# Post-norm linear attention with a butterfly FFN: x first in the load queue, contraction weights transposed in slot 13, epsilon on VectorE, one norm applied by ScalarE

## What is computed

```python
q, k, v = split(x @ W_qkv)                    # 16 heads of 64
q, k = relu(q @ W_f + b_f), relu(k @ W_f + b_f)
kv = einsum('bhnd,bhne->bhde', k, v)
o = einsum('bhnd,bhde->bhne', q, kv) / (einsum('bhnd,bhd->bhn', q, k.sum(axis=2)) + 1e-6)
x = layernorm(x + merge(o) @ W_out + b_out)   # eps 1e-5
h = butterfly(x @ W_exp + b_exp, up_weights)  # 512 wide, 9 stages of 2x2 blocks
h = butterfly(gelu(h + up_bias), down_weights)
x = layernorm(x + h @ W_con + b_con + down_bias)
```

## Time and profile before

| | us |
|---|---|
| median of 3 runs | 331.06 (330.26 to 331.89) |
| the profiled execution | 331.18 |
| its span | 329.4 |
| TensorE busy in it | 309.8 |
| VectorE busy | 244.9 |
| ScalarE busy | 153.3 |
| GpSimd busy | 105.8 |

### The profile page before, as it was taken

One profiled execution on the slowest core, in us unless ns is written; L12 is line 12 of the kernel. 1 busy time (PEld: TensorE's weight loads), 2 busy tenths in 40 slices (PEclk: granted clock), 3 DMA queues, 4 the chain that ended last, 5 costly groups with the idle time before them and its releaser, 6 DMA issues.

```text
span 329.4 us, 5508 instructions
## 1 busy us (share of the span) xinstructions
PE 309.8 (94%) x2009; PEld 233.5 (71%) x2009; DVE 244.9 (74%) x479; ACT 153.3 (47%) x273; POOL 105.8 (32%) x111
## 2 busy tenths in 40 slices
PE   5899799999989999999999999999999898999992
PEld 4666476776757777677678777777797686769892
DVE  2568999869599899788892896669747843757845
ACT  2633235444643453555362456336647846330440
POOL 4058999990000002300210033004402602423523
PEclk9999999999999999999999999999999999999999
DMA  6993335376900840460047011900191182372012
GB/s 180 245 335 98 112 127 190 119 214 155 224 0 6 196 85 1 111 150 0 3 113 148 0 35 45 215 1 0 38 225 33 37 206 52 95 169 61 1 34 64
DMA packets 25762, 33.95 MB, mean 103 GB/s; under 512 B 3944, under 2 KB 14600, under 8 KB 25736
## 3 DMA queue, kind: packets, MB, share of 16 engines
q1 hardware_dynamic: 25576, 33.57, 40.0%
q10 hardware_dynamic: 160, 0.03, 0.0%
HBM read 31.24 MB, written 2.36 MB: 102 GB/s over the span
## 4 chain that ended last, share of the span: by engine, by line
PE 71%; DVE 11%; DMA 5%; issue 4%; SPq 3%; ACT 3%; POOL 2%; POOLq 0%; DVEq 0%; ACTq 0%
PE ring L642 26%; PE kx_ps L729 13%; PE attn_ps L642 8%; PE spare_ps L832 7%; PE ring L749 4%; DMA x<-_L_ffn_down_weights_dram 3%; PE desk L651 2%; PE desk L763 2%; DMA bf_col<-in_L_attn_b_f_dram 2%; PE desk L738 2%; PE ring L709 2%; SPq L489 1%; DVE late L1195 1%; POOL rstd L587 1%; DVE qn L1309 1%
## 5 line engine op out<-in xcount | busy, mean ns | idle before, releaser
L1011 ACT ACTIVATE q<-ring,bf_col 128x512 f32<-128x512 f32 x64 | 43.8, 684 | 42.4 <-PE ring L642 41.8
L581 POOL TENSOR_TENSOR var_eps<-mean_var,ln_eps 128x4 f32<-128x4 f32 x14 | 7.1, 504 | 169.9 <-DVE mean_var L1322 169.9
L729 PE MATMUL kx_ps<-k,xs 128*128 128x512 f32 x128 | 60.1, 592 | 0.0
L1309 DVE TENSOR_TENSOR qn<-q,recips 128x512 f32<-128x512 f32 x64 | 42.4, 701 | 2.1 <-DMA recips<-recip_rows 2.1
L997 ACT ACTIVATE qn_h<-qn 128x512 fp32r<-128x512 f32 x48 | 29.5, 625 | 30.1 <-DVE qn L1309 30.1
L564 POOL TENSOR_TENSOR y<-hid,y_up 128x512 f32<-128x512 f32 x18 | 33.6, 1889 | 17.1 <-DMA hid<-in_L_ffn_up_weights_dram 16.1
L729 PEld LDWEIGHTS kx_ps<-k,xs 128*128 128x128 f32 x128 | 23.9, 189 | 17.9 <-issue 15.4
L642 PE MATMUL ring<-xT_h,wq_h 128*128 128x512 f32 x64 | 35.6, 556 | 0.2 <-ACT hid L1074 0.2
L1177 DVE TENSOR_TENSOR qn_l<-qn,qn_h 128x512 fp32r<-128x512 f32 x48 | 32.2, 679 | 4.3 <-ACT qn_h L997 4.1
L1275 DVE TENSOR_TENSOR k_total<-k_total,k 128x1024 f32<-128x1024 f32 x24 | 35.1, 1461 | 0.3
L1249 DVE TENSOR_TENSOR k<-ring,bf_minus 128x512 f32<-128x512 f32 x32 | 21.9, 684 | 14.2 <-PE ring L642 14.1
(11 more groups left out here) (174 smaller groups left out, 595.8 us busy)
## 6 DMA issues: line engine op xcount, KB each, us to landing
recips<-recip_rows SPq DMA_DIRECT2D x64, 256.0 KB, 5.5
hid<-in_L_ffn_up_weights_dram SPq DMA_DIRECT2D x9, 512.0 KB, 3.9
x<-_L_ffn_down_weights_dram SPq DMA_DIRECT2D x9, 512.0 KB, 6.6
xs<-in_L_attn_x_dram SPq DMA_DIRECT2D x4, 512.0 KB, 6.4
out_dram<-y SPq DMA_DIRECT2D x7, 256.0 KB, 2.3
q<-in_L_attn_W_qkv_dram SPq DMA_DIRECT2D x2, 512.0 KB, 8.1
q<-in_L_attn_W_qkv_dram SPq DMA_DIRECT2D x2, 256.0 KB, 3.3
q<-in_L_attn_W_out_dram SPq DMA_DIRECT2D x2, 256.0 KB, 8.9
```

What stands on the lines that cost most here:

```text
L729: t_.matmul(kx_ps[half], xs[b % XBUF][:, t, :], k[kt % KRING][:, half * CH:(half + 1) * CH], start=t == 0, stop=t == TILES - 1).then_inc(s ...
L1011: a_.activation(q[:, i % QRING, :], bank(("q", i))[:, :], ACT.Relu, bias=bf_col[:, :])\
L1309: v.tensor_tensor(qn[:, a % NRING, :], q[:, a % QRING, :], recips[:, a % PAIRS // RC, a % RC, :], ALU.mult).then_inc(s_qn, 1)
```

## The change

1. Loads: the first chunk of x is loaded ahead of the k weights, the second after SyncE has waited for the second half of the k weights. A partition takes four tokens that lie side by side (2 KB in one piece, in place of four pieces of 512 bytes); the output is stored in the same order (2 KB pieces, 1 KB for the halves of the last chunk). All x loads have the new order. `bf_row` is loaded through ScalarE's queue, and the two loads of `bf_col` stand behind the load of x for sequence 1, with a semaphore of their own that the first q relu waits for.
2. TensorE's first work: see the rows below. ScalarE's and VectorE's first work follows that order.
3. ScalarE, not VectorE, copies the transposed v weights in slots 1 and 2.
4. `down_step` 8 stands in slot 12 (was 10); its result is transposed on the desk and copied to `wdn` in slot 13 (was 16).
5. Epsilon, and the negated mean where it is needed, are made by VectorE right behind `bn_aggr`.
6. In the slot of the last norm product (277 us) the first attention step stands ahead of it.
7. The second LayerNorm of chunk 6 is applied by ScalarE after its last gelu (VectorE before, ahead of its work on the last chunk). Chunk 7 has statistics tiles of its own.

```diff
-    DOWN_STEP_SLOT = {1: 0, 2: 1, 3: 2, 5: 3, 6: 4, 7: 5, 8: 6, 9: 7, 10: 8}
+    WDN_SLOT = 13
+    DOWN_STEP_SLOT = {1: 0, 2: 1, 3: 2, 5: 3, 6: 4, 7: 5, 8: 6, 9: 7, 12: 8}
+    BY_ACT = [[n for s, n in ATT_T_SLOT.items() if s < APPLY_END],
+              [n for s, n in Y_SLOT.items() if s < APPLY_END] + [LAST - 1]]
-    xs_view = x.rearrange("b (t p) c -> b p t c", p=128)
-    out_view = out.rearrange("b (h t p) c -> (b h) p t c", p=128, h=CHUNKS)
+    xs_view = x.rearrange("b (h p t) c -> b p h t c", p=128, h=CHUNKS)
+    out_view = out.rearrange("b (h p t) c -> (b h) p t c", p=128, h=CHUNKS)
...
+            load_x(0, slice(0, 1), s_xs0)
             for half in range(2):
                 cols = slice(HD + half * CH, HD + (half + 1) * CH)
                 sp.dma_start(wqkv_raw[:, cols], W_qkv[:, cols]).then_inc(s_wk[half], 16)
-            sp.dma_start(xs[0][:, :, :], xs_view[0, :, :, :]).then_inc(s_xs[0], 16)
-            sp.dma_start(bf_row[:, :], b_f.rearrange("(o n) -> o n", o=1).to_broadcast([128, D])).then_inc(s_bf, 16)
+            sp.wait_ge(s_wk[1], 16)
+            load_x(0, slice(1, 2), s_xs[0])
             weights(0, s_wq)
-            for h in range(2):
-                sp.dma_start(bf_col[h * D:(h + 1) * D, :], b_f.rearrange("(p o) -> p o", o=1)).then_inc(s_bf, 16)
...
-                pool.wait_ge(s_mv[i], QUADS * (n + 1))
-                g.tensor_tensor(var_eps[i][:, :], mean_var[i][:, :, 1], ln_eps[:, :].to_broadcast([128, QUADS]),
-                                ALU.add).then_inc(s_ve[i], 1)
...
+                for a in adds(s)[:1]:
+                    add_attn(a)
                 if s in LATE_NORM_SLOT:
                     norm(LATE_NORM_SLOT[s])
-                for a in adds(s)[:1]:
-                    add_attn(a)
...
+                if s in V_SLOT:
+                    act.wait_ge(s_dmade, desk_of["v", V_SLOT[s]] + 1)
+                    a_.activation(wT[:, (4 + V_SLOT[s]) * CH:(5 + V_SLOT[s]) * CH], desk[:, :],
+                                  ACT.Copy).then_inc(s_dtaken, 1)
...
+            layer_norm_apply(1, LAST - 1, y[:, (LAST - 1) % 2, :, :], s_yo)
...
+                dve.wait_ge(s_mv[i], QUADS * (n + 1))
+                v.tensor_scalar(var_eps[i][:, :], mean_var[i][:, :, 1], LN_EPS, 1.0, ALU.add,
+                                ALU.mult).then_inc(s_ve[i], 1)
+                if n in BY_ACT[i]:
+                    v.tensor_scalar(mean_minus[i][:, :], mean_var[i][:, :, 0], -1.0, 0.0, ALU.mult,
+                                    ALU.add).then_inc(s_mm[i], 1)
...
-            layer_norm_end(1, LAST - 1, y[:, (LAST - 1) % 2, :, :], s_yo)
```

More of the change, by code:

```diff
@@ L274, in postln_linear_attention_butterfly_ffn_kernel @@
         x1T_l = sb("x1T_l", [128, CH], fp32r)
[L275 to L278, removed]
+        stats = [sb(f"stats{i}", [128, QUADS, 6]) for i in range(3)]
+        mean_var = [sb(f"mean_var{i}", [128, QUADS, 2]) for i in range(3)]
+        var_eps = [sb(f"var_eps{i}", [128, QUADS]) for i in range(3)]
+        rstd = [sb(f"rstd{i}", [128, QUADS]) for i in range(3)]
         mean_minus = [sb(f"mean_minus{i}", [128, QUADS]) for i in range(2)]
@@ L380, in postln_linear_attention_butterfly_ffn_kernel @@
         s_atc = sem("attn_copied")
[L381 to L384, removed]
+        s_st = [sem(f"stats_{i}_done") for i in range(3)]
+        s_mv = [sem(f"mean_var_{i}_done") for i in range(3)]
+        s_ve = [sem(f"var_eps_{i}_done") for i in range(3)]
+        s_rs = [sem(f"rstd_{i}_done") for i in range(3)]
+        s_mm = [sem(f"mean_minus_{i}_done") for i in range(2)]
         s_of = [sem(f"offset_{i}_done") for i in range(2)]
@@ L465, in _ @@
             load_down(0)
-            sp.dma_start(xs[1][:, :, :], xs_view[1, :, :, :]).then_inc(s_xs[1], 16)
+            load_x(1, slice(0, CHUNKS), s_xs[1])
+            for h in range(2):
+                sp.dma_start(bf_col[h * D:(h + 1) * D, :], b_f.rearrange("(p o) -> p o", o=1)).then_inc(s_bfc, 16)
             load_down(1)
@@ L864, in _ @@
             fold_wf(3, spare_ps)
[L865 to L871, removed]
+            pe.wait_ge(s_wh, 1)
+            pe.wait_ge(s_wl, 1)
             for s in range(SLOTS):
@@ L1075, in gelu @@
                     .then_inc(s_taken, 1)
+            act.wait_ge(s_xp, 1)
+            hi(xT_h[:, 0, 0:CH], kx_ps[0], s_xTh)
             act.wait_ge(s_wT, 1)
             a_.activation(wT[:, 2 * CH:3 * CH], ring[0][:, :], ACT.Copy).then_inc(s_wTa, 1)
-            for half, fold in enumerate([attn_ps, spare_ps]):
-                act.wait_ge(s_fold, half + 1)
-                hi(wk_h[:, half * CH:(half + 1) * CH], fold[:, :], s_wh)
-            act.wait_ge(s_xp, 1)
-            hi(xT_h[:, 0, 0:CH], kx_ps[0], s_xTh)
-            act.wait_ge(s_bf, 48)
+            act.wait_ge(s_fold, 1)
+            hi(wk_h[:, 0:CH], attn_ps[:, :], s_wh)
+            act.wait_ge(s_bf, 16)
             act.wait_ge(s_bfz, 1)
@@ L1121, in _ @@
                 if s == 0:
-                    for half, fold in enumerate([attn_ps, spare_ps]):
+                    act.wait_ge(s_wT, 3)
+                    a_.activation(wT[:, CH:2 * CH], attn_ps[:, :], ACT.Copy).then_inc(s_wTa, 1)
+                    k_relu(1, 0)
+                    for half, fold in enumerate([spare_ps, attn_ps]):
                         act.wait_ge(s_fold, half + 3)
@@ L1432, in _ @@
                     layer_norm_end(1, Y_SLOT[s], y[:, Y_SLOT[s] % 2, :, :], s_yo)
-                if s in V_SLOT:
-                    dve.wait_ge(s_dmade, desk_of["v", V_SLOT[s]] + 1)
-                    v.tensor_copy(wT[:, (4 + V_SLOT[s]) * CH:(5 + V_SLOT[s]) * CH], desk[:, :]).then_inc(s_dtaken, 1)
                 if s == WCON_SLOT:
@@ L1448, in _ @@
                     bias_row_step(st)
+                if s == WDN_SLOT:
+                    dve.wait_ge(s_dmade, desk_of["wdn",] + 1)
+                    v.tensor_copy(wdn[:, :, :].rearrange("p a c -> p (a c)"), desk[:, :]).then_inc(s_dtaken, 1)
                 if s == BIAS_T_SLOT:
```

102 lines of the change are left out of this document (58 added, 44 removed).

## The result

The changed kernel took 329.16 us (median of 11 runs, 327.75 to 331.22); the kernel before, run on the same chips, 331.89 (11 runs, 329.72 to 335.33). The ratio is 0.992, with a 95% interval from 0.990 to 0.995: faster, by 2.7 us. The forecast was 326.5 with a range from 324.0 to 328.9, so the time lies outside it and the gain is little more than half of the 4.65 forecast. (The forecast was laid on an execution of 331.18; laid on the 331.89 of the kernel before here, the same gain would have given 327.2, still 1.9 too low.) The profiled execution took 328.99, its span is 327.2 (329.4 before): 2.2 us less.

What follows compares the result with a forecast made beforehand. The prediction took TensorE, busy 309.8 of 329.4 us, to bound the kernel. Its terms, 2.5 + 1.4 + 0.45 - 0.4 + 0.7 = 4.65 us off an execution of 331.18, gave 326.5 us, range 324.0 to 328.9.

Steps and rivals of the forecast that it cites:

- TensorE ready for `ksum`: Slot 14: TensorE would reach ksum at 109.0 us, against 112.77 in the kernel before.
- the new wait there: At ksum of slot 14, TensorE would wait about 1.2 us for VectorE, which copies wdn until 110.2.
- early at `ksum`: Slot 14: counted through VectorE alone, TensorE would be early by 112.77 - 110.2 = 2.5 us.
- slot 16: The transposition of wdn at 135.06 and the wait behind it, to 136.44, both go: 1.4 us gained.
- epsilon in the middle: Epsilon on VectorE, 0.23 to 0.4 us per norm, lies in time TensorE doesn't wait for: taken as nothing.
- late norm order: Attention step ahead of the last norm product fills TensorE's 0.87 us wait at 277.44; 0.45 us gained, bounds 0 and 0.9.
- epsilon ahead of the first half norm: Three epsilon additions on VectorE before chunk 7's first half norm (311.49), which TensorE waits for: 0.4 us lost.
- the end: VectorE takes chunk 7 without first applying chunk 6's norm, and a GpSimd wait shrinks by 0.3: 0.7 us gained.
- TensorE stays at half speed: Rival on the start: doubled product spacing lasts on, to 26 us for a measurable loss, 332.8 us; chance 0.05.
- the 1.0 of the start: Start: 1.4 us of waits removed, less a load-queue gap, taken as 1.0; said not to enter the time at ksum.
- Step 5: VectorE's down-butterfly step, waiting for its load, would start 0.8 us earlier than 70.48, at about 69.7.
- rival C: Slower case: doubled spacing of TensorE's products in the start lasts until 26 us, giving 332.8 us; chance 0.05.

Runs made afterwards that it cites:

- e1: Changed kernel with the transposition and copy of wdn in slot 15 in place of 13; 326.88 us (4 runs), ratio to the kernel before 0.986.
- e3: Changed kernel with both the desk wait and the thin products of slot 14's ksum moved behind the second k product; 326.16 us (4 runs).
- e2: Changed kernel with the desk wait left in place, but the 16 thin products of slot 14's ksum behind the second k product; 328.13 us (4 runs).
- e4: Changed kernel with epsilon and the negated mean made by GpSimd, as in the kernel before; 327.49 us (10 runs).
- e8: Changed kernel without SyncE's wait for the k weights ahead of the second chunk of x; 332.88 us (one run).
- e10: Changed kernel with the v weights copied off the desk by VectorE again, in place of ScalarE; 335.62 us (one run).
- e7: Changed kernel with x and the output in the old token order, pieces of 512 bytes in every load and store; 330.18 us (one run).
- e11: Kernel before with only step 8 moved to slot 12 and wdn to slot 13; 336.26 us (one run).
- e6: Changed kernel with VectorE's copy of wdn ahead of the bias step in slot 13, to shorten the wait at ksum; 328.50 us (one run).
- e5: Changed kernel with wdn in slot 15 and epsilon on GpSimd; 325.15 us (4 runs), ratio to the kernel before 0.978.
- e9: Changed kernel with slot 14's desk wait and thin ksum products behind the second k product, and epsilon on GpSimd; 324.69 us (5 runs), ratio 0.977.

## Why the prediction was wrong, step by step

| step | forecast | measured |
|---|---|---|
| TensorE ready for `ksum` (a time) | 109.0 | 108.56 |
| the new wait there (in the next row) | 1.2 | 1.51 |
| early at `ksum` | 2.5 | 2.70 |
| fall of the clock behind it | 0 | -1.70 |
| slot 16 | +1.4 | +1.48 |
| epsilon in the middle | 0 | -0.93 |
| late norm order | +0.45 | +0.39 |
| epsilon ahead of the first half norm | -0.4 | -0.46 |
| the end | +0.7 | +0.72 |
| sum | 4.65 | 2.2 |

From the third row on, each measured value is the difference of one instruction's start in the two traces, less the difference at the instruction of the row above.

**The step that failed** is the one with the new wait: "TensorE is early by 112.77 - 110.2 = 2.5". The time of `ksum` was right (110.07 for 110.2 and 0.1 of semaphore); what it is worth was not: of the 2.70 us 1.0 was left at the transposition of the bias. I charged the wait only for its length, as if TensorE went on behind it as fast as before. It went on at half clock for 3.4 us from 113.2 on. A row to suspect it was there: in the start the second fold takes 1.22 us where the first takes 1.92, and the rival "TensorE stays at half speed" used just that. I did not ask whether the speed can drop again at the wait that I was adding. e1 and e3 took the wait away and the fall went with it, and e2 shows that what stands next to the wait counts. With this term the sum is 2.95. The Trainium skill (TensorE: Matmul & The Clock Gate, HAM oscillation) tells of a kernel in which TensorE waits for loads between bursts of products, is throttled by it, and starts the next burst cold. The traces here agree that the clock can fall after a wait; but these waits were of 0.6 to 1.5 us and for a copy, and the clock fell 0.6 to 3.1 us behind them, not at the first product. Why thin products next to the wait matter, and why some executions of e4 escape, stays open.

**The second step** is "I take nothing" for epsilon in the middle. I argued from "TensorE stands nowhere in 160 to 250 us", but the cover of a VectorE operation is VectorE's own slack, and VectorE's rows show no wait from 214.8 to 231.4 and from 248.4 to 262 us. TensorE then waits for it, 0.20 at 227.18 and 0.29 at 252.03: the prediction had named such waits (between 140 and 250 us) as a sign that it is wrong. The price of a norm was in my numbers (0.23 to 0.4; it is 0.27 here); the collision with GpSimd wasn't. e4 gives back 0.4 by 227 us and 1.0 by 261; the 0.93 of the table is what the two traces lose against each other between 143 and 262 us.

**Right for a wrong reason.** The wait at `ksum` came out at nearly the forecast length, and I wrote "this value comes from VectorE alone: the 1.0 of the start doesn't enter it". It does. VectorE in the changed kernel (lines far apart, between 68 and 110 us):

```profile
68.20 1.16 DVE L1221 TENSOR_TENSOR late<-x,spare_ps 128x512 f32<-128x512 f32 x1 [2.07 <-DMA x<-_L_ffn_down_weights_dram]
...
80.19 1.29 DVE L1335 TENSOR_TENSOR qn<-q,recips 128x512 f32<-128x512 f32 x2 [1.03 <-DMA recips<-recip_rows]
...
94.28 0.69 DVE L1275 TENSOR_TENSOR k<-ring,bf_minus 128x512 f32<-128x512 f32 x1 [1.04 <-PE ring L651]
...
96.50 0.95 DVE L1319 RECIPROCAL recip<-recip 128x128 f32<-128x128 f32 x1 [0.33 <-ACT recip L1066]
...
109.35 0.67 DVE L1480 COPY wdn<-desk 128x512 f32<-128x512 f32 x1
```

Step 5 stood at 68.20, 1.5 earlier than I had it, and the reciprocals' step 1.7 earlier; then, without step 8 in slot 10, VectorE caught up and waited 1.04 for TensorE at 94.28. From the reciprocal of slot 12 it has 12.8 us of work to the copy of `wdn` in every trace that has the copy at that place (96.50 to 109.35; 98.77 to 111.61 in e8; 101.51 to 114.34 in e10), and TensorE has 1.5 less to `ksum`. So the wait is 1.5 whenever TensorE comes: with the start 2.3 later (e8) it is 1.52, with slot 2 slower (e10) 1.50. Nor does the load of step 5 set it: step 5 stood at 68.20 in the changed kernel, at 69.68 in e4 and at 71.10 in e7, and the wait was 1.51, 1.48 and 1.58. My count came near because two errors met. So in the changed kernel what the start gains or loses reaches the end in full (2.3 later in e8, at `ksum` too), which the forecast denied.

**The other steps held.** The start gave 1.2 in this trace. Over the nine traces with the new order and 2 KB pieces (e8 left out) the mean to W_con is 18.7, over the three of the old one 19.7: 1.0, as forecast, within a spread of over 1 us. Most of the spread is that of the spacing in the first products, which halves at about 7 us in some executions, at about 10 in others and in between in the rest (second fold 1.07 us long in the changed kernel, 1.90 in e1). What rival C feared, then, happens in some executions, but up to 10 us and not 26, for 0.65 us. ScalarE's v copies removed the wait and, with it, the falls of slot 2 that e10 and e11 show; that may be part of why the runs of the kernel before reach 335 (those with a mean clock up to 0.993 took 332.4 to 335.3, those from 0.995 on 330.7 to 332.4), but no trace of before holds such a fall, so this stays open. Of the two sides of step 8's move, e11 gives the sum in one run: alone it is a loss.

## What to carry to other kernels

A wait of TensorE is not priced by its length alone. Look at what stands next to it: 0.6 to 1.5 us of wait right ahead of thin products cost another 1.7 to 3.3 in every trace here, though not in every run, and the same 1.5 us of wait with wide products behind it cost nothing more. Where a new wait can't be avoided, try to put work with many columns between it and the thin part, or let independent products pass ahead of the wait. And a small operation is only free on an engine with slack of its own; whether the engine that waits for it stands now is the wrong question.

## What the runs showed of the hardware

- The granted clock fell not in the wait but behind it: 3.1 us after its end in the changed kernel (110.07 to 113.2), 3.0 in e4, 2.7 in e6, 1.5 in e7, 0.6 to 1.4 in e8, e10 and e11. So the first slow product is not where the cause stands. The falls lasted 3.3 to 3.4 us (changed kernel, e4, e6, e7) or 6.8 (e8, e10, e11), and cost half of that, 1.7 or 3.3.
- In slot 2, where no thin products stand, two traces with waits of 1.72 and 2.20 us had no fall, and two with waits of 2.27 and 2.47 had one (1.6 us each). So a wait can do it without thin products too. I draw no limit from four cases.
- The fall is not certain. Of the changed kernel's runs ten of eleven have a mean clock of 0.994 or less; the one with 0.999, which can't hold a fall of 3.4 us, is the fastest, 327.75 us. Of e4's ten, four can't hold it either. Of the 21 runs without the wait next to thin products (e1, e2, e3, e5, e9), 20 can't, and one reads 0.995.
- A 128x512 subtraction of VectorE took 1.75 us beside a GpSimd addition on SBUF, and 0.69 without.
